# A four-layer attention and expert kernel on one core: the start reordered. Weight loads, folds and the normalisation of three contexts

## The chip, the cores and the metric

One core of one Trainium2 chip runs the whole program. The metric is the device time of one execution in microseconds, taken as the median of several runs. The engines are named as the profile names them: PE is TensorE (PEld its weight loads), DVE is VectorE, ACT is ScalarE, POOL is GpSimd, SP is SyncE, which here only issues DMAs.

## The reference, cut to what matters

Four sublayers follow each other on `x` (16 sequences of 128 tokens, 256 wide), each added to `x` after a layer norm: a cross attention on a context (16 x 128 x 192), a slot feed-forward, a second cross attention with 16 heads, and a mixture of 8 experts. Only the first one is touched by the change:

```python
def _L0_xattn_ref(modality1, modality2, ln1_g, ln1_b, ln2_g, ln2_b, Wq, bq, Wk, bk, Wv, bv, Wo, bo):
    ...
    x1 = layernorm(modality1, ln1_g, ln1_b)
    x2 = layernorm(modality2, ln2_g, ln2_b)
    q = x1 @ Wq + bq
    k = x2 @ Wk + bk
    v = x2 @ Wv + bv
    scores = jnp.einsum('bqe,bke->bqk', q, k) * scaling
    attn = jax.nn.softmax(scores, axis=-1)
    ctx = jnp.einsum('bqk,bke->bqe', attn, v)
    return ctx @ Wo + bo
...
x = x + _L0_xattn_ref(_layernorm(x, axis=-1), ctx_768, ...)
```

## The kernel before, in words

All of it is fp32. The 16 sequences are worked in four groups of four (`g` 0 to 3). Each group's rows `X[g]` and context `CH[g]` come by one DMA each; DVE takes mean and variance, POOL the power -0.5 (`root`), DVE normalises; PE transposes rows and context (`turn_x`, `turn_context`), ACT copies the transposes out of PSUM.

**Folding.** Weights that follow each other are multiplied once at the start: `Wq Wk^T` becomes `qk` (`fold_query`), `Wv Wo` becomes `vo` (`fold_value`), and the biases and the norm's gains go with them. So a group's attention is `query` (rows times `qk`, evicted by ACT to `Q`), `score` against the normalised context, softmax, `value` and `attend`. `fold_query` on PE has two parts that are interleaved by half: 256-column products of `WqT` and `WkT` into PSUM bank 4, and one-column products of `Wq` with the bias column `ln1_b` (from `keep`) into bank 5. `fold_query_bias` multiplies the result of the latter, `u_col`, by `WkT`. `fold_value` likewise has 256-column products of `WvT` and `Wo` and one-column ones of `Wv`.

**Order.** There is no planner. Each engine's program is a list of calls written out by hand in its block, and engines meet by semaphores. SP's list (L335 to L350) issues the loads in the order in which the queue shall work on them: the three matrices of the query fold (`WqT`, `WkT`, `Wq`: 768 KB), the first piece of `keep` (identity, ones, columns: 149.5 KB), the rows of group 0, the three of the value fold (768 KB), then contexts and rows by turns. The semaphore of each load is in the call. The counters `fold_ps` (PE has finished a fold) and `fold_ok` (DVE has read it out of PSUM and written it) count the folds in the order of the lists.

**PE's list (L1301 on).** It begins with `idle(5)`: five 128x256 matmuls on a zeroed tile `blank` whose results nobody reads. Then it waits for `keep`, runs `fold_query`, `fold_value`, one more idle matmul, `turn_x(0)`, `fold_query_bias`, `query(0)`, `fold_slot_values`, `turn_context(0)`, `turn_x(1)`, `fold_value_bias`, `score(0)`, `query(1)`, `value(0, 0)`, `turn_context(1)`, `turn_probs(0)`, `fold_slot_bias`, `turn_x(2)`, `score(1)` and so on. The helper `mm` (L923) records all matmuls, `turn` (L927) all transposes, so blocks are told apart by tiles and counts: an fp32 matmul is two records of MATMUL (and two of LDWEIGHTS), a 128x128 transpose one. A block of four 256-column matmuls is "128x256 x8"; it is what `fold_slot_values` (18.03 us) and `value` are; the 16 records at 19.84 us are `turn_context(0)` and `turn_x(1)`.

**DVE's list (L2131 on).** `stats_x(0)`, `fold_query` (the column `u_col`), `norm_x(0)`, `stats_c(0)`, `fold_query_bias` (the column `q_col`), `stats_x(1)`, `norm_c(0)`, `norm_x(1)`, `fold_value`, `stats_c(1)`, `fold_slots`, `most(0)`, `fold_value_bias`, `norm_c(1)`, `stats_x(2)`, `stats_c(2)`, `norm_x(2)`, `stats_c(3)`, `fold_slot_bias`, `most(1)`, `stats_x(3)`, `norm_c(2)`, and later `norm_c(3)`. `norm` (L1611) is four `tensor_scalar` instructions with a mean and a factor for each row of the tile.

**POOL's list (L444 on).** A few memsets, then nothing but `root` until 125 us; ahead of the second attention it has `spread_keys`.

**ACT's list (L712 on).** It waits for `keep`, fills `spread`, then `fold_query` (scales `qk` out of PSUM), `rows_turned(0)` (L545), `query(0)` (L565), `context_turned(0)` (L549), and so on.

The functions that the diff touches, as they stand before:

Of the kernel before, what the change touches and what calls it, by code (L numbers as in the profile page):

```python
# [61 lines left out]
])  # L62
FOLD_A, FOLD_B, FOLD_C = FOLD["Wo"][0], FOLD["fwv"][0], FOLD["whh"][0]
ROWS, ROWS_N = columns([
# [4 lines left out]
def build(nc, x_d, ctx_d, ctxT_d, keep_d, fold_d, rows_d, w13_d, w2_d, xh_d, early_d, out_d):  # L69
    with ExitStack() as stack:  # L70
# [3 lines left out]
        def sem(name):  # L74
            return stack.enter_context(nc.semaphore(name))
# [158 lines left out]
        keep_in, fold_in, rows_in = sem("keep_in"), sem("fold_in"), sem("rows_in")  # L234
        keep_in2, keep_in3, fold_in2, fold_in3, fold_in4 = (sem(t) for t in ("keep_in2", "keep_in3", "fold_in2", "fold_in3", "fold_in4"))
        x_in = [sem(f"x_in{g}") for g in range(NG)]
        c_in = [sem(f"c_in{g}") for g in range(NG)]
# [72 lines left out]
        def _(sp):  # L310
# [23 lines left out]

            some_fold(0, FOLD_A, fold_in)  # L335
            some_keep(0, KEEP_A, keep_in)
            rows_of(0)
            some_fold(FOLD_A, FOLD_B, fold_in2)
# [49 lines left out]
        def _(pool):  # L388
            def root(g, name):
                pool.wait_ge(s["var_" + name], g + 1)  # L390
                v = var["c" if name == "ch" else "x", g]
                pool.tensor_tensor(v[:, :], v[:, :], minus_half[:, :], ALU.pow).then_inc(s["rs_" + name], 1)  # L392

            def spread_keys(u):
# [57 lines left out]
            root(1, "xh")  # L452
            root(1, "ch")
            root(2, "xh")
            root(2, "ch")
            root(3, "ch")
            root(0, "xh2")
            root(3, "xh")
# [461 lines left out]
        def _(pe):  # L920
# [332 lines left out]
            def fold_query():  # L1253
                pe.wait_ge(fold_in, 16)
                for m in range(KD):
                    mm(ps[:, 4, m * D:(m + 1) * D], [(WqT[:, k, m * P:(m + 1) * P], WkT[:, k, :]) for k in range(KD)])
                    ins = mm(ps[:, 5, m:m + 1], [(Wq[:, k, m * P:(m + 1) * P], kept("ln1_b")[:, k:k + 1]) for k in range(KD)])
                ins.then_inc(fold_ps, 1)
# [6 lines left out]

            def fold_value():
                pe.wait_ge(fold_in2, 16)
                for m in range(KD):
                    mm(ps[:, 6, m * D:(m + 1) * D], [(WvT[:, k, m * P:(m + 1) * P], Wo[:, k, :]) for k in range(KD)])
                    ins = mm(ps[:, 7, 8 + m:9 + m], [(Wv[:, k, m * P:(m + 1) * P], kept("ln2_b")[:, k:k + 1]) for k in range(KD)])  # L1270
                ins.then_inc(fold_ps, 1)

# [28 lines left out]
            pe.wait_ge(set_ok, 2)  # L1301
            idle(5)
            pe.wait_ge(keep_in, 16)
            fold_query()
            fold_value()
            idle(1)
            turn_x(0)
            fold_query_bias()
            query(0)
            fold_slot_values()  # L1310
            turn_context(0)
            turn_x(1)
            fold_value_bias()
            score(0)
            query(1)
# [284 lines left out]
        def _(dve):  # L1600
# [33 lines left out]
            def norm_c(g):  # L1634
                norm(g, CH[g], CH[g], DC, "ch")
# [438 lines left out]
            def fold_query_bias():  # L2074
                dve.wait_ge(fold_ps, 3)
                dve.tensor_tensor(q_col[:, :], ps[:, 7, 0:KD], kept("ln2_g"), ALU.mult)
                folded()
# [65 lines left out]
            fold_value_bias()  # L2143
            norm_c(1)
            stats_x(2)
# [5 lines left out]
            stats_x(3)  # L2151
            norm_c(2)
            add_attention(0, 0)
# [3 lines left out]
            norm_x2(0)  # L2157
            norm_c(3)
            add_attention(1, 0)
# [288 lines left out]
```

## Time and profile before

| | |
|---|---|
| median of 3 runs | 548.62 us (548.39 to 549.3) |
| the profiled execution's own time | 548.08 us |
| its span, first to last instruction | 546.3 us, mean granted clock 0.999 |
| busy: PE, PEld, DVE, ACT, POOL | 97%, 80%, 52%, 47%, 31% of the span |
| DMA | 74.30 MB, mean 136 GB/s |

The profile is of one execution. Busy time is the sum of an engine's instructions; for PE their ends are modelled, so that two consecutive blocks overlap by about the length of one instruction in the rows, and the distance from start to start is the time that a block takes. A timeline row merges consecutive instructions of one kind and gives the start, the length, and in brackets the idle time before it with what ended it.

### The profile page before, as it was taken

To read this page: it belongs to the slowest core of one execution; us is meant where nothing else is said; L and a number is where in the kernel's file an instruction comes from. 1 tells how busy PE (TensorE), PEld (TensorE's weight loads), DVE (VectorE), ACT (ScalarE), POOL (GpSimd) and SP (SyncE) were. 2 spreads that over 40 slices of the span, in tenths; PEclk is the share of its full clock that TensorE was granted. 3 is DMA by queue.
4 is the path that set the end of the run, shared out by engine and by line. 5 is a ranking of instruction groups with operands and counts; after the bars stand their busy time and mean duration, and the time that the engine had idled before them with its cause. 6 is when DMAs were issued, how large, how long until landed. Compare 5 with 4: busy or idle time off the path is not lost.

```text
span 546.3 us, 11013 instructions
## 1 busy us (share of the span) xinstructions
PE 532.3 (97%) x3939; PEld 438.2 (80%) x3940; DVE 282.3 (52%) x843; ACT 255.3 (47%) x591; POOL 168.4 (31%) x152
## 2 busy tenths in 40 slices
PE   8999999999999999999999799999999999999996
PEld 7687878767555677767777589999999999999995
DVE  3886777988442776855788765722212121212110
ACT  2433676453356766688787825532221212222221
POOL 2221000102063221342222053345344444444423
PEclk9999999999999999999999999999999999999999
DMA  9930000000120000300460667978888888888832
GB/s 311 396 135 2 2 0 2 1 1 1 38 67 1 2 2 1 117 1 2 157 268 7 232 207 259 273 213 279 206 268 220 255 223 250 227 246 231 241 66 29
DMA packets 29083, 74.30 MB, mean 136 GB/s; under 512 B 5648, under 2 KB 20368, under 8 KB 23920
## 3 DMA queue, kind: packets, MB, share of 16 engines
q1 hardware_dynamic: 19456, 62.27, 32.4%
q0 software_dynamic: 7488, 10.39, 11.2%
q10 hardware_dynamic: 2096, 1.08, 0.7%
q8 instruction: 25, 0.41, 0.3%
q14 instruction: 18, 0.15, 0.1%
HBM read 62.88 MB, written 10.85 MB: 135 GB/s over the span
## 4 chain that ended last, share of the span: by engine, by line
PE 91%; ACT 3%; DVE 2%; DMA 1%; issue 1%; DVEq 0%; POOL 0%; SPq 0%
PE ps L923 62%; PE ps L1226 12%; PE ps L927 11%; PE ps L1074 1%; PE ps L1083 1%; DMA ring<-in_fold 1%; PE ps L1086 1%; ACT ring L645 1%; PE ps L1077 1%; PE ps L1014 1%; PE ps L1057 1%; ACT ring L652 1%; ACT ring L686 0%; ACT HF L657 0%; DVE arena L1615 0%
## 5 line engine op out<-in xcount | busy, mean ns | idle before, releaser
L923 PE MATMUL ps<-keep,arena 128*128 128x128 f32 (+2 forms) x976 | 114.9, 274 | 0.0
L923 PEld LDWEIGHTS ps<-keep,arena 128*128 128x128 f32 x976 | 112.8, 192 | 1.5 <-issue 1.1
L2053 DVE TENSOR_TENSOR keep<-keep,ps 128x512 f32<-128x512 f32 x39 | 26.8, 688 | 147.9 <-PE ps L923 139.9
L441 POOL DMA_INDIRECT out_x<-arena,row_no x38 | 59.9, 1576 | 101.1 <-ACT arena L704 82.3
L1226 PE MATMUL ps<-arena,keep 128*128 x312 | 73.7, 380 | 0.1
L693 ACT COPY keep<-ps 128x256 f32<-128x256 f32 x39 | 14.5, 372 | 105.5 <-PE ps L927 105.5
L400 POOL TENSOR_TENSOR ring<-arena,keep 128x512 f32<-128x512 f32 x32 | 33.4, 1047 | 97.0 <-PE ps L923 79.8
L1226 PEld LDWEIGHTS ps<-arena,keep 128*128 128x128 f32 x312 | 56.4, 190 | 6.6 <-issue 0.3
L645 ACT ACTIVATE ring<-ps,mx 128x128 f32<-128x128 f32 x192 | 52.1, 403 | 6.2 <-DVE mx L1753 6.2
L923 PE MATMUL ps<-ring,arena 128*32 128x128 f32 (+1 forms) x640 | 53.1, 348 | 1.5 <-ACT ring L652 1.4
L392 POOL TENSOR_TENSOR var_x<-var_x,minus_half 128x4 f32<-128x4 f32 x16 | 16.6, 1041 | 110.1 <-DVE var_x L1609 110.1
L923 PE MATMUL ps<-arena,keep 128*128 128x256 f32 (+1 forms) x144 | 44.2, 454 | 0.5 <-ACT arena L599 0.5
L652 ACT COPY ring<-ps 128x1024 f32<-128x1024 f32 x32 | 33.2, 1039 | 16.5 <-PE ps L927 15.9
L697 ACT ACTIVATE keep<-ps 128x512 f32<-128x512 f32 x39 | 23.3, 596 | 35.7 <-PE ps L923 35.6
L1753 DVE TENSOR_REDUCE mx<-ps 128x8 f32<-128x1024 f32 x24 | 29.2, 1216 | 17.9 <-PE ps L923 17.7
L927 PEld LDWEIGHTS ps<-keep,ring 128*128 128x128 f32 x256 | 28.2, 141 | 11.8 <-issue 8.4
L923 PE MATMUL ps<-keep,w_first 128*128 128x128 f32 x320 | 37.7, 275 | 0.0
L923 PEld LDWEIGHTS ps<-keep,w_first 128*128 128x128 f32 x320 | 36.7, 192 | 0.1
L923 PEld LDWEIGHTS ps<-ring,arena 128*32 128x32 f32 (+1 forms) x640 | 22.6, 124 | 17.3 <-issue 14.3
L923 PEld LDWEIGHTS ps<-arena,keep 128*128 128x128 f32 x144 | 26.4, 190 | 12.4 <-issue 9.5
L927 PE MATMUL ps<-keep,ring 128*128 128x128 f32 x256 | 34.2, 277 | 1.4 <-ACT arena L662 1.1
L428 POOL DMA_INDIRECT keep<-normed,row_no x30 | 30.3, 1010 | 10.9 <-issue 8.2
(266 smaller groups left out, 802.1 us busy)
## 6 DMA issues: line engine op xcount, KB each, us to landing
arena<-in_w SPq DMA_DIRECT2D x29, 1024.0 KB, 5.2
w_first<-in_w SPq DMA_DIRECT2D x10, 1024.0 KB, 5.3
arena<-in_w SPq DMA_DIRECT2D x8, 512.0 KB, 7.3
keep<-in_keep SPq DMA_DIRECT2D x1, 2827.0 KB, 17.0
ring<-in_fold SPq DMA_DIRECT2D x3, 768.0 KB, 7.0
arena<-in_x SPq DMA_DIRECT2D x4, 512.0 KB, 9.2
arena<-in_ctxT SPq DMA_DIRECT2D x4, 512.0 KB, 10.2
arena<-in_ctx SPq DMA_DIRECT2D x4, 384.0 KB, 9.4
```

What stands on the lines that cost most here:

```text
L392: pool.tensor_tensor(v[:, :], v[:, :], minus_half[:, :], ALU.pow).then_inc(s["rs_" + name], 1)
L400: pool.tensor_tensor(KB[u % 2], KT[g][:, t, bb * S:(bb + 1) * S].unsqueeze(1).broadcast_to([P, HT4, S]), kept("head_mask").unsqueeze(2).br ...
L428: pool.indirect_dma_start(out=XI[t % DEEP], out_offset=None, in_=early_d if t < EARLY else xh_d, in_offset=bass.IndirectOffsetOnAxis(ap=ro ...
L441: pool.indirect_dma_start(out=out_d, out_offset=bass.IndirectOffsetOnAxis(ap=rows_at, axis=0), in_=YO[t % DEEP], in_offset=None, compute_o ...
L645: ins = act.activation(PP[u % 2][:, h, :], scores_of(u)[:, h, :], ACT.Exp, bias=mx[u % 2][:, h:h + 1], scale=1.0)
L652: act.copy(PQ[u % 2], ps[:, 4:6, :].rearrange("p t (h n) -> p (t h) n", h=4)).then_inc(s["pt"], 1)
L697: act.activation(HA[r % 2], ps[:, 2 * (r % 2), :], ACT.Silu).then_inc(silu, 1)
L923: ins = pe.matmul(out, w, m, start=(k == 0), stop=(k == len(pairs) - 1))
L927: return pe.transpose(out, t, ident)
L1226: ins = pe.matmul(Y_PS[r % 2], HA[r % 2][:, k * P:(k + 1) * P], w2e[:, bass.ds(at + k * D, D)], start=(k == 0), stop=(k == INTER // P - 1))
L1753: dve.tensor_reduce(mx[u % 2][:, :], scores_of(u), AXX, ALU.max, negate=True).then_inc(s["neg"], 1)
L2053: dve.tensor_tensor(HA[r % 2], HA[r % 2], ps[:, 2 * (r % 2) + 1, :], ALU.mult).then_inc(act_ok, 1)
```

## The change

- **Loads.** The first fold load is cut in two: `WqT` and `WkT` (512 KB) go first, then the rows of group 0, then the first piece of `keep`, then `Wq` (256 KB, its own semaphore `fold_in_u`). The rest of SP's order stays.
- **The query fold on PE** is cut the same way: `fold_query` has only the 256-column products and waits only for the first load; `fold_query_row` has the one-column products, waits for `keep` and `fold_in_u`, and counts `fold_ps`.
- **The value fold on PE** is two calls: half `m=0` ahead of `turn_x(0)`, half `m=1` behind `query(0)`, with a wait for `fold_ok` 2 (DVE has read `q_col` from the same bank). DVE's `fold_query_bias` waits for `fold_ps` 2 now, since the value fold is counted third.
- **PE's order**: idle(4), `fold_query`, idle(1), `fold_query_row`, idle(2), `fold_value(0)`, `turn_x(0)`, `fold_query_bias`, `query(0)`, `fold_value(1)`, `turn_context(0)`, `turn_x(1)`, `fold_slot_values`, `score(0)`, `fold_value_bias`, `query(1)`; from there as before.
- **Contexts 1 to 3** are normalised on POOL, right behind their `root`, no longer on DVE.

```diff
@@ -60,7 +60,7 @@
     ("WqT", KD * D), ("WkT", KD * D), ("Wq", KD * D), ("Wo", KD * D), ("WvT", KD * D), ("Wv", KD * D),
     ("fwv", KD * D), ("fwoT", KD * D), ("slots", KD * NSLOT), ("whh", KD * 3 * D),
 ])
-FOLD_A, FOLD_B, FOLD_C = FOLD["Wo"][0], FOLD["fwv"][0], FOLD["whh"][0]
+FOLD_U, FOLD_A, FOLD_B, FOLD_C = FOLD["Wq"][0], FOLD["Wo"][0], FOLD["fwv"][0], FOLD["whh"][0]
 ROWS, ROWS_N = columns([
     ("bo", D), ("slot_scale", NSLOT), ("b2", NSLOT), ("tau", 1), ("fbo", D), ("ab2", D),
 ])
@@ -233,6 +233,7 @@
 
         keep_in, fold_in, rows_in = sem("keep_in"), sem("fold_in"), sem("rows_in")
         keep_in2, keep_in3, fold_in2, fold_in3, fold_in4 = (sem(t) for t in ("keep_in2", "keep_in3", "fold_in2", "fold_in3", "fold_in4"))
+        fold_in_u = sem("fold_in_u")
         x_in = [sem(f"x_in{g}") for g in range(NG)]
         c_in = [sem(f"c_in{g}") for g in range(NG)]
         y_in = [sem(f"y_in{g}") for g in range(NG)]
@@ -332,9 +333,10 @@
             def some_fold(lo, hi, landed):
                 sp.dma_start(ring[:, lo:hi], fold_d[:, lo:hi]).then_inc(landed, 16)
 
-            some_fold(0, FOLD_A, fold_in)
+            some_fold(0, FOLD_U, fold_in)
+            rows_of(0)
             some_keep(0, KEEP_A, keep_in)
-            rows_of(0)
+            some_fold(FOLD_U, FOLD_A, fold_in_u)
             some_fold(FOLD_A, FOLD_B, fold_in2)
             context_rows_of(0)
             rows_of(1)
@@ -391,6 +393,13 @@
                 v = var["c" if name == "ch" else "x", g]
                 pool.tensor_tensor(v[:, :], v[:, :], minus_half[:, :], ALU.pow).then_inc(s["rs_" + name], 1)
 
+            def norm_c(g):
+                pool.wait_ge(s["rs_ch"], g + 1)
+                for t in range(GB):
+                    ins = pool.tensor_scalar(CH[g][:, t, 0:DC], CH[g][:, t, 0:DC], mv["c", g][:, t, 0:1], var["c", g][:, t:t + 1],
+                                             ALU.subtract, ALU.mult)
+                ins.then_inc(s["ch"], 1)
+
             def spread_keys(u):
                 g, bb, t = u // UNITS, u // 2 % GB, u % 2
                 if u % UNITS == 0:
@@ -451,9 +460,12 @@
             root(0, "ch")
             root(1, "xh")
             root(1, "ch")
+            norm_c(1)
             root(2, "xh")
             root(2, "ch")
+            norm_c(2)
             root(3, "ch")
+            norm_c(3)
             root(0, "xh2")
             root(3, "xh")
             root(1, "xh2")
@@ -1254,6 +1266,11 @@
                 pe.wait_ge(fold_in, 16)
                 for m in range(KD):
                     mm(ps[:, 4, m * D:(m + 1) * D], [(WqT[:, k, m * P:(m + 1) * P], WkT[:, k, :]) for k in range(KD)])
+
+            def fold_query_row():
+                pe.wait_ge(keep_in, 16)
+                pe.wait_ge(fold_in_u, 16)
+                for m in range(KD):
                     ins = mm(ps[:, 5, m:m + 1], [(Wq[:, k, m * P:(m + 1) * P], kept("ln1_b")[:, k:k + 1]) for k in range(KD)])
                 ins.then_inc(fold_ps, 1)
 
@@ -1263,12 +1280,14 @@
                     ins = mm(ps[:, 7, m:m + 1], [(WkT[:, k, m * P:(m + 1) * P], u_col[:, k:k + 1]) for k in range(KD)])
                 ins.then_inc(fold_ps, 1)
 
-            def fold_value():
+            def fold_value(m):
                 pe.wait_ge(fold_in2, 16)
-                for m in range(KD):
-                    mm(ps[:, 6, m * D:(m + 1) * D], [(WvT[:, k, m * P:(m + 1) * P], Wo[:, k, :]) for k in range(KD)])
-                    ins = mm(ps[:, 7, 8 + m:9 + m], [(Wv[:, k, m * P:(m + 1) * P], kept("ln2_b")[:, k:k + 1]) for k in range(KD)])
-                ins.then_inc(fold_ps, 1)
+                if m:
+                    pe.wait_ge(fold_ok, 2)
+                mm(ps[:, 6, m * D:(m + 1) * D], [(WvT[:, k, m * P:(m + 1) * P], Wo[:, k, :]) for k in range(KD)])
+                ins = mm(ps[:, 7, 8 + m:9 + m], [(Wv[:, k, m * P:(m + 1) * P], kept("ln2_b")[:, k:k + 1]) for k in range(KD)])
+                if m:
+                    ins.then_inc(fold_ps, 1)
 
             def fold_slot_values():
                 pe.wait_ge(fold_in3, 16)
@@ -1299,19 +1318,21 @@
                 ins.then_inc(fold_ps, 1)
 
             pe.wait_ge(set_ok, 2)
-            idle(5)
-            pe.wait_ge(keep_in, 16)
+            idle(4)
             fold_query()
-            fold_value()
             idle(1)
+            fold_query_row()
+            idle(2)
+            fold_value(0)
             turn_x(0)
             fold_query_bias()
             query(0)
-            fold_slot_values()
+            fold_value(1)
             turn_context(0)
             turn_x(1)
+            fold_slot_values()
+            score(0)
             fold_value_bias()
-            score(0)
             query(1)
             value(0, 0)
             turn_context(1)
@@ -2072,7 +2093,7 @@
                 folded()
 
             def fold_query_bias():
-                dve.wait_ge(fold_ps, 3)
+                dve.wait_ge(fold_ps, 2)
                 dve.tensor_tensor(q_col[:, :], ps[:, 7, 0:KD], kept("ln2_g"), ALU.mult)
                 folded()
 
@@ -2141,7 +2162,6 @@
             fold_slots()
             most(0)
             fold_value_bias()
-            norm_c(1)
             stats_x(2)
             stats_c(2)
             norm_x(2)
@@ -2149,13 +2169,11 @@
             fold_slot_bias()
             most(1)
             stats_x(3)
-            norm_c(2)
             add_attention(0, 0)
             add_attention(0, 1)
             gather_stats(0, "xh2")
             fold_state()
             norm_x2(0)
-            norm_c(3)
             add_attention(1, 0)
             most(2)
             add_attention(1, 1)
```

## Rows read from the trace of the kernel before

**Rows 1.** Top of the page: the span, and the busy time of each engine

```profile
span 546.3 us, 11013 instructions
...
PE 532.3 (97%) x3939; PEld 438.2 (80%) x3940; DVE 282.3 (52%) x843; ACT 255.3 (47%) x591; POOL 168.4 (31%) x152
```

**Rows 2.** What TensorE waited for in 0 to 50 us: total, times, longest (us)

```profile
PE ps L927 <- DVE arena L1615: 0.8, 1, 0.8
...
PE ps L923 <- DMA ring<-in_fold: 0.8, 1, 0.8
```

**Rows 3.** Busy time by engine in 33 to 95 us, granted clock, DMA share, GB/s

```profile
33.00:95.00 62.00, 61.96 (x367) 50.30 (x368) 45.27 (x175) 34.23 (x70) 5.19 (x6) 1.00 0.01 1
```

**Rows 4.** DMA issues, first weight transfer and first rows: KB, us to landing

```profile
ring<-in_fold SPq DMA_DIRECT2D x1, 768.0 KB, 4.4
...
arena<-in_x SPq DMA_DIRECT2D x1, 512.0 KB, 5.5
```

**Rows 5.** Timeline to 15 us, SP's first issue and TensorE: start, length, instructions

```profile
0.73 0.39 SPq L333 DMA_DIRECT2D ring<-in_fold  x1
...
1.26 4.54 PE L923 MATMUL ps<-blank 128*128 128x256 f32 x10 [1.26 <-POOL blank L446]
...
5.60 0.73 PEld L923 LDWEIGHTS ps<-ring 128*128 128x128 f32 x4 [0.43 <-DMA keep<-in_keep]
...
9.13 0.73 PEld L923 LDWEIGHTS ps<-ring 128*128 128x128 f32 x4 [0.84 <-DMA ring<-in_fold]
...
11.75 0.30 PEld L923 LDWEIGHTS ps<-blank 128*128 128x128 f32 x2
...
12.08 1.01 PEld L927 LDWEIGHTS ps<-keep,arena 128*128 128x128 f32 x8
...
14.49 0.30 PEld L923 LDWEIGHTS ps<-arena,qk 128*128 128x128 f32 x2 [0.46 <-issue]
```

**Rows 6.** Timeline, VectorE and ScalarE on the first group of rows

```profile
7.15 1.40 DVE L1622 BATCH_NORM_STATS2 stat_x<-arena 128x6 f32<-128x256 f32 x4 [7.15 <-DMA arena<-in_x]
...
10.41 1.38 DVE L1615 TENSOR_SCALAR arena<-arena,mv_x,var_x 128x256 f32<-128x256 f32 x4 [0.84 <-POOL var_x L392]
...
13.37 1.01 ACT L545 COPY arena<-ps 128x1024 f32<-128x1024 f32 x1 [4.11 <-PE ps L927]
...
18.30 1.45 ACT L565 ACTIVATE arena<-ps,q_col,keep 128x512 f32<-128x512 f32 x2 [3.92 <-PE ps L923]
```

**Rows 7.** Timeline, TensorE from 18 to 34 us

```profile
18.03 1.89 PE L923 MATMUL ps<-ring 128*128 128x256 f32 x8
...
19.84 1.94 PE L927 MATMUL ps<-keep,arena 128*128 128x128 f32 x16
...
21.62 1.03 PE L923 MATMUL ps<-ring,spread 128*128 128x256 f32 x4
...
22.48 1.95 PE L923 MATMUL ps<-arena 128*128 128x128 f32 x16
...
24.27 3.60 PE L923 MATMUL ps<-arena,qk 128*128 128x512 f32 x8
...
33.04 1.09 PE L927 MATMUL ps<-keep,arena 128*128 128x128 f32 x8 [0.78 <-DVE arena L1615]
```

**Rows 8.** Timeline, VectorE around the second context's normalisation

```profile
24.47 0.69 DVE L1648 TENSOR_REDUCE nm<-ps 128x4 f32<-128x512 f32 x1 [0.34 <-PE ps L923]
...
26.71 1.24 DVE L1615 TENSOR_SCALAR arena<-arena,mv_c,var_c 128x192 f32<-128x192 f32 x4
...
31.61 1.38 DVE L1615 TENSOR_SCALAR arena<-arena,mv_x,var_x 128x256 f32<-128x256 f32 x4
```

**Rows 9.** GpSimd: two square roots in the timeline, and a group of the page

```profile
22.79 1.01 POOL L392 TENSOR_TENSOR var_c<-var_c,minus_half 128x4 f32<-128x4 f32 x1 [5.05 <-DVE var_c L1609]
...
31.78 1.25 POOL L392 TENSOR_TENSOR var_c<-var_c,minus_half 128x4 f32<-128x4 f32 x1 [0.73 <-DVE var_c L1609]
...
L400 POOL TENSOR_TENSOR ring<-arena,keep 128x512 f32<-128x512 f32 x32 | 33.4, 1047 | 97.0 <-PE ps L923 79.8
```

## The prediction, made before the changed kernel was run

> **What bounds the kernel now.** The page comes first: TensorE is busy for 532.3 of 546.3 us [rows 1]. A change to the start can only bring what TensorE loses there, so the next view is what it waited for in the first 50 us: 0.8 us for the transposes of the third group of rows, where VectorE was late, and 0.8 us for the value fold's weights [rows 2]. The timeline adds 0.43 us ahead of the query fold, where `keep` was late, 0.46 us ahead of `query(0)`, and idle matmuls: five at the start, one at 11.75 us [rows 5]. That is about 2.5 us of waits and 0.4 us of filler after 5.6 us; everything from 33 to 95 us is full: 61.96 us of 62.00 [rows 3]. Two questions decide: how many of these waits go, and what new ones the new order makes. I follow TensorE from block to block; a block costs the distance from its start to the next one's.
>
> **Prices.** Four 256-column matmuls: 19.84 - 18.03 = 1.81 us; sixteen transposes: 21.62 - 19.84 = 1.78; `fold_value_bias`: 22.48 - 21.62 = 0.86; `score`: 24.27 - 22.48 = 1.79 [rows 7]. The whole value fold is 11.75 - 9.13 = 2.62, so half of it is 1.31 and the one-column products of a fold are 2.62 - 1.81 = 0.81. `query(0)` is 18.03 - 14.49 = 3.54 [rows 5, 7]. An idle matmul takes 4.54 / 5 = 0.9 at the start, where TensorE runs at half its later pace, and 0.33 (weight loads) to 0.5 later; I take 0.43 [rows 5].
>
> **The loads.** 768 KB landed at 0.73 + 4.4 = 5.13, `keep` at 5.60, the rows at 1.65 + 5.5 = 7.15 [rows 4 to 6]. 512 KB of rows thus took 7.15 - 5.60 = 1.55 us. The first piece is now 256 KB shorter and lands about 0.8 earlier, at 4.4. The rows have 405.5 KB less ahead of them, 1.2 us: they land at 5.95. `keep` follows at 6.4 and `Wq` at 7.2. The value weights have the same bytes ahead of them as before and stay at 9.13. SP's one more issue costs 0.39 [rows 5]; the queue still has bytes to move, so I count it at nothing. Without that cover all later loads come 0.4 later.
>
> **TensorE to the value fold.** idle(4) ends at 1.26 + 0.8 x 4.54 = 4.9; the fold weights are there. `fold_query` starts then, at half pace until 5.6 (where the pace rose before), so 0.7 us do 0.35 of its 1.81, and it ends at 7.05. idle(1) 7.5; `fold_query_row` finds its weights, 8.3; idle(2) 9.15. `fold_value(0)` can start at 9.13 as before. So the 0.43 and 0.8 of waits have turned into filler and gained nothing by themselves. What is gained is that only half of the value fold stands ahead of the rows: TensorE is free at 10.45.
>
> **The first rows.** VectorE and GpSimd need 10.41 + 1.38 - 7.15 = 4.64 us from landing to `norm_x(0)`'s end [rows 6]; the two bias instructions fit in the wait for the root as before, since `fold_query_row` is done at 8.3. So the rows are ready at 10.6, and `turn_x(0)` starts there, not at 12.08 [rows 5]. From its start to `query(0)` were 14.49 - 12.08 = 2.41 us, of which ACT's copy and the turns are the chain and `fold_query_bias` lies beside [rows 5, 6]. `query(0)` starts at 13.0, 1.5 earlier. This is the change's real gain.
>
> **What comes late next.** `turn_context(0)` waits for `Q`, which ACT had 18.30 + 1.45 - 14.49 = 5.26 after `query(0)` began [rows 5, 6]: 18.25 now. TensorE has been free of `query(0)` since 16.55, and the only filling is `fold_value(1)`, 1.31, to 17.85. A new wait of 0.4 us stands where `fold_slot_values` (1.81) covered it fully. `fold_value(1)` itself waits for `fold_ok` 2; VectorE has then only `stats_c(0)` and the column behind it to do after 10.6, and 6 us for it. `turn_context(0)` starts at 18.25 against 19.84, 1.6 earlier [rows 7].
>
> **The debts.** Then come 1.78 (turns), 1.81 (`fold_slot_values`, moved behind), 1.79 (`score(0)`): `score(0)` ends at 23.65 against 24.27; `fold_value_bias` 0.86: `query(1)` starts at 24.5 against 24.27 [rows 7]. The 1.6 is spent: 1.31 on the deferred half of the fold, 0.4 on the new wait. Up to here the change is worth nothing, or costs 0.2.
>
> **GpSimd's share.** VectorE's list loses `norm_c(1)`, 1.24 us, from 26.71 to where `stats_x(2)` begins [rows 8]. `most(0)` starts with the end of `score(0)`, 0.65 earlier (24.47 before). So `norm_x(2)`, which ended at 31.61 + 1.38 = 32.99, ends at 32.99 - 0.65 - 1.2 = 31.15 [rows 8]. TensorE would be ready for `turn_x(2)` at 33.04 - 0.78 + 0.2 = 32.45 [rows 7], so its wait of 0.78 is gone and the start is 0.6 earlier than 33.04. GpSimd's four instructions aren't in the trace. Lower bound: VectorE's own, 1.24 for the four [rows 8]. Upper: the 128x512 product of two tensors, 1.047 each, 4.2 [rows 9]. I take 1.6, nearer the first because they are 192 wide with one tensor read. `root(1, "ch")`, at 22.79 before, starts near 21.7, since the value fold on VectorE starts when `fold_value(1)` ends and not at 19. `norm_c(1)` is then done between 23.9 and 26.9; `turn_context(1)` stands behind `query(1)` (3.4) and `value(0, 0)` (1.8), at 29.7: covered at either bound. Behind it on GpSimd's queue is `root(2, "xh")`, due near 28: also free. `norm_c(2)` and `norm_c(3)` replace VectorE work (some 2.5 us) in a stretch where TensorE doesn't wait [rows 3]: nothing.
>
> **One rule against it.** While VectorE ran `norm_x(2)`, GpSimd's root took 1.25 us, not 1.01, and VectorE's four took 1.38, as at 10.41 us where GpSimd was idle [rows 6, 8, 9]: in these rows only GpSimd pays. By them the sum keeps its 0.6. The Trainium skill, SBUF — State Buffer, "Who interferes with whom", says that the port pair which VectorE shares with GpSimd is an exclusive lock: whoever issues first holds it for a whole instruction and the other fully blocks. By that rule, VectorE could be the one that waits; that is the second rival.
>
> **The sum.** 0.6 us from 548.08 is 547.5 for a profiled execution; the median of the runs shown is 0.54 above the profiled one, so I expect a median of 548.62 - 0.6 = 548.0. A measurement of this kernel can tell about 0.2% (1.1 us) from no change: this is "same". The forecast's own range is a gain of 0 to 1.0.
>
> **Rivals.**
> 1. Faster. VectorE is relieved of 3.7 us (three times 1.24) and the new order closes the 0.4 us wait: the gain is 0.6 + 0.4, and up to 0.5 more if stalls behind the modelled ends of matmuls were VectorE's. Gain 1.0 to 1.5, 547.3. For it: TensorE at 97% hides small waits in its rows [rows 1]. Against: rows 3 are full, and `Q`'s chain is ACT's.
> 2. Slower, by the lock. If GpSimd's `norm_c` runs beside `norm_x(2)`, each of its four instructions may wait for one of GpSimd's, up to 1.047 [rows 9]: 4.2 us. `norm_x(2)` has 32.45 - 31.15 = 1.3 us of slack, so it decides from there and costs up to 2.9; net 2.3 slower, 550.9. Against: `norm_c(1)` would have to last until 29.8, 1.8 us each, and `norm_c(2)` starts only behind `root(2, "ch")`, near 31.3, when `norm_x(2)` is done.
> 3. Slower, by the clock. The profile prints a granted clock of 1.00 throughout [rows 3], but the first idle matmuls took twice the later time [rows 5]. If the pace rises one such stretch later in the new order, at about 10 us, the work from 5.6 on takes double: 1.46 + 0.4 + 0.8 + 0.9 ends near 11.3, not 9.15, and all after it moves by 2.0: net 1.4 slower, 550.0. It decides once the pace rises after 6. Against: TensorE is at work from 1.26 on in both.
> 4. The rows land no earlier, since transfers share the queues. Then `turn_x(0)` starts at 11.8 and everything behind moves by 1.2: 0.6 slower than before, 549.2.
>
> **Chances.** The forecast 0.60, rival 1 0.22, rival 4 0.08, rivals 2 and 3 0.05 each. Rival 1 is the only one below -0.2%, rivals 2 and 3 lie above +0.2%: faster 0.22, same 0.68, slower 0.10. The range goes from rival 1's middle, 547.0, to rival 4, 549.3; what is left out is the rest of rival 1 and rivals 2 and 3.
>
> **What would show it.** Right: rows landing near 6.0; `query(0)` near 13.0; a wait of some 0.4 for ACT ahead of `turn_context(0)`; `query(1)` within 0.3 of 24.27; `turn_x(2)` near 32.4 without a wait; GpSimd's instructions at 0.3 to 1.0 us. Wrong: a wait ahead of `turn_context(1)` or `turn_x(2)`, long VectorE instructions in `norm_x(2)`, idle matmuls at 0.9 after 6 us, or a difference that first appears after 33 us.

## The result, and the profile after

The changed kernel takes 548.02 us (median of 22 runs, 547.63 to 548.57) against 548.62 us (22 runs) before: ratio 0.9983, 95% interval 0.9977 to 0.9990. The medians differ by 0.60 us, less than the 0.2% that the prediction calls "same"; the ratio is one of means and stands for 0.9 us, since a few runs before took up to 551.23. Its profiled execution took 547.71 us. The top of its page, against [rows 1]:

```profile
span 545.9 us, 11019 instructions
...
PE 532.5 (98%) x3941; PEld 438.3 (80%) x3942; DVE 279.1 (51%) x831; ACT 255.5 (47%) x591; POOL 180.6 (33%) x164
```

VectorE has 3.2 us less to do, GpSimd 12.2 us more; TensorE has what it had, in 0.4 us less.

The landings first. DMA issues of the changed kernel, each from a window around its issue: the query fold's two matrices (issued at 0.74), the rows (1.19), `keep` (1.66), `Wq` (2.20), the value fold's weights (2.7); size and microseconds to landing.

```profile
ring<-in_fold SPq DMA_DIRECT2D x1, 512.0 KB, 4.1
...
arena<-in_x SPq DMA_DIRECT2D x1, 512.0 KB, 5.1
...
keep<-in_keep SPq DMA_DIRECT2D x1, 149.5 KB, 5.1
...
ring<-in_fold SPq DMA_DIRECT2D x1, 256.0 KB, 5.2
...
ring<-in_fold SPq DMA_DIRECT2D x1, 768.0 KB, 6.7
```

They land at 4.8, 6.36, 6.8, 7.4 and 9.4 us. What TensorE waited for in the first 50 us, to be held against [rows 2]:

```profile
PE ps L939 <- issue: 0.4, 1, 0.4
PE ps L935 <- ACT arena L557: 0.4, 1, 0.4
PE ps L935 <- DMA ring<-in_fold: 0.2, 1, 0.2
PE ps L939 <- DVE arena L1636: 0.2, 1, 0.2
```

And its timeline, with the instructions that decide on the other engines (start, length, instructions, idle time before):

```profile
4.88 1.59 PEld L935 LDWEIGHTS ps<-ring 128*128 128x128 f32 x8 [0.56 <-DMA ring<-in_fold]
...
9.42 0.73 PEld L935 LDWEIGHTS ps<-ring 128*128 128x128 f32 x4 [0.28 <-DMA ring<-in_fold]
...
11.07 0.86 PEld L939 LDWEIGHTS ps<-keep,arena 128*128 128x128 f32 x8 [0.27 <-DVE arena L1636]
...
13.33 0.30 PEld L935 LDWEIGHTS ps<-arena,qk 128*128 128x128 f32 x2 [0.46 <-issue]
...
17.14 1.45 ACT L577 ACTIVATE arena<-ps,q_col,keep 128x512 f32<-128x512 f32 x2 [3.92 <-PE ps L935]
...
18.68 1.94 PE L939 MATMUL ps<-keep,arena 128*128 128x128 f32 x16 [0.45 <-issue]
...
23.12 4.00 POOL L399 TENSOR_SCALAR arena<-arena,mv_c,var_c 128x192 f32<-128x192 f32 x4
...
24.84 3.60 PE L935 MATMUL ps<-arena,qk 128*128 128x512 f32 x8
...
30.22 1.38 DVE L1636 TENSOR_SCALAR arena<-arena,mv_x,var_x 128x256 f32<-128x256 f32 x4
...
32.67 1.04 PE L939 MATMUL ps<-keep,arena 128*128 128x128 f32 x8
```

Read it against [rows 5 to 8]. `turn_x(0)` starts at 11.07 (12.08 before) and `query(0)` at 13.33 (14.49). ACT finishes `Q` at 18.59, and `turn_context(0)` starts at 18.68, after 0.45 us in which TensorE has nothing to do: the new wait. (The bracket says "issue", that is, the view names no releaser; that it is `Q` follows from the code, where `turn_context(0)` waits for it, from the time, and from e3 below, where other work fills the gap.) `query(1)` then starts at 24.84 where it started at 24.27, so the reordering has cost 0.57 us by there. `turn_x(2)` has no bracket: VectorE was done with `norm_x(2)` at 31.60, and the 0.78 us wait at 33.04 is gone. From the next block on the shift is constant. `score(1)`, and `gate_r(1)` of the slot layer, which stands behind ACT's copy of the second group's shares, first in the changed kernel, then before:

```profile
33.54 1.95 PE L935 MATMUL ps<-arena 128*128 128x128 f32 x16
...
95.34 1.99 PE L935 MATMUL ps<-arena,keep 128*128 128x256 f32 x8 [0.46 <-ACT arena L611]
```

```profile
33.97 1.95 PE L923 MATMUL ps<-arena 128*128 128x128 f32 x16
...
95.78 1.99 PE L923 MATMUL ps<-arena,keep 128*128 128x256 f32 x8 [0.46 <-ACT arena L599]
```

That is 0.43 and 0.44 us. I use the second row, `gate_r(1)`, below as the mark of what a start is worth.

### The profile page after: what moved, and what is told of

Read it like the earlier page. It is cut to its first block, busy times and chain, and to the rows that moved or that the text cites. A ratio compares the mean times of both kernels' runs of the same rounds, so it can differ in the third digit from the quotient of the medians.

```text
span 545.9 us, 11019 instructions
## 1 busy us (share of the span) xinstructions
PE 532.5 (98%) x3941; PEld 438.3 (80%) x3942; DVE 279.1 (51%) x831; ACT 255.5 (47%) x591; POOL 180.6 (33%) x164
## 4 chain that ended last, share of the span: by engine, by line
PE 91%; ACT 4%; DVE 2%; issue 1%; DMA 1%; POOL 0%; DVEq 0%; SPq 0%
PE ps L935 62%; PE ps L1238 12%; PE ps L939 11%; ACT ring L657 2%; PE ps L1086 1%; PE ps L1095 1%; DMA arena<-in_x 1%; ACT ring L664 1%; PE ps L1098 1%; PE ps L1089 1%; PE ps L1026 1%; PE ps L1069 1%; ACT HF L669 0%; ACT ring L698 0%; PE ps L1167 0%
## 5 line engine op out<-in xcount | busy, mean ns | idle before, releaser
L1774 DVE TENSOR_REDUCE mx<-ps 128x8 f32<-128x1024 f32 x24 | 29.2, 1216 | 17.5 <-PE ps L935 17.3
```

The lines of the kernel that those rows point to most:

```text
L1774: dve.tensor_reduce(mx[u % 2][:, :], scores_of(u), AXX, ALU.max, negate=True).then_inc(s["neg"], 1)
```

## Experiments

Each kernel's times are compared with runs of the kernel before on the same chip in the same session; its median there lay between 548.45 and 549.06. Where two kernels come from different sessions, the difference of their medians is therefore uncertain by some tenths. I then compare what each gains on the kernel before in its own session (0.60 for the changed kernel), and the marks. A mark is one execution, and the first loads alone land up to 0.25 us earlier or later from one profile to the next.

### The two halves of the change, each alone

```diff
@@ e1, against the kernel before: only GpSimd's part
             root(1, "ch")
+            norm_c(1)
             root(2, "xh")
             root(2, "ch")
+            norm_c(2)
             root(3, "ch")
+            norm_c(3)
...
-            norm_c(1)
...
-            norm_c(2)
...
-            norm_c(3)
```

(and GpSimd's function `norm_c` as in the change).

> The kernel before, with one part of the change: GpSimd normalises contexts 1 to 3; loads, folds and TensorE's order stay as they were. Theory A (the reordering is worth nothing or less, the gain is the 0.78 us wait ahead of turn_x(2) that VectorE's relief removes): turn_x(2)'s weight loads start at 31.9 us, where TensorE is free, and not at 33.04; score(1) follows at 32.9 and not 33.87, so the kernel is 1.0 us faster than before (547.6) and 0.4 faster than the whole change. Theory B (the gain is the earlier first query): 0.0 to 0.2 us faster than before, with a wait somewhere ahead of 33 us that takes the place of the one removed. Theory C (GpSimd's four take 4.0 us instead of 1.24 and make turn_context(1) or the root of x2 late): slower than before, with a wait for POOL.

547.51 us, ratio 0.9969 (0.9956 to 0.9983); against the 548.87 of the same session it is 1.4 us faster, against the 548.62 above 1.1. Its timeline, TensorE, `query(1)`, `turn_x(2)` and the mark:

```profile
24.04 3.60 PE L933 MATMUL ps<-arena,qk 128*128 128x512 f32 x8
...
31.87 1.04 PE L937 MATMUL ps<-keep,arena 128*128 128x128 f32 x8
...
94.55 1.99 PE L933 MATMUL ps<-arena,keep 128*128 128x256 f32 x8 [0.46 <-ACT arena L609]
```

The mark is 1.23 us earlier than before and 0.79 earlier than in the changed kernel. (0.2 of it are loads that happened to land earlier: the value fold's matmuls started at 8.91, and 9.14 before.) Without them the removed wait is worth 1.0 us. This one part of the change, alone, is worth about twice the whole.

```diff
@@ e2, against the changed kernel: the reordering without GpSimd's part
-            norm_c(1)
...
-            norm_c(2)
...
-            norm_c(3)
@@ and on VectorE's list
             fold_value_bias()
+            norm_c(1)
             stats_x(2)
```

(`norm_c(2)` and `norm_c(3)` go back to their places too.)

> The changed kernel with the contexts' normalisation back on VectorE: the reordering alone. Theory A: query(1)'s weight loads at 24.6 us as in the changed kernel (24.16 before), norm_x(2) ends 1.2 later than the changed kernel's 31.6, so turn_x(2) waits for VectorE until 32.9 and starts 0.1 earlier than before; time within 0.2 us of before (548.6). Theory B: it keeps the whole 0.6 us of the change (548.0).

548.22 us, ratio 0.9989 (0.9980 to 0.9998), 0.65 faster than before in its session: the number of theory B, though not by way of an earlier `query(1)`. VectorE and TensorE around `turn_x(2)`, then the mark:

```profile
26.28 1.24 DVE L1626 TENSOR_SCALAR arena<-arena,mv_c,var_c 128x192 f32<-128x192 f32 x4
...
31.18 1.38 DVE L1626 TENSOR_SCALAR arena<-arena,mv_x,var_x 128x256 f32<-128x256 f32 x4
...
32.61 1.09 PE L929 MATMUL ps<-keep,arena 128*128 128x128 f32 x8
...
95.34 1.99 PE L925 MATMUL ps<-arena,keep 128*128 128x256 f32 x8 [0.46 <-ACT arena L601]
```

The mark stands at 95.34, exactly where the whole change has it. I had expected VectorE to hold `turn_x(2)` until 32.9. It was done at 32.56, because `score(0)` comes earlier in the new order and `most(0)` with it, just when TensorE, 0.6 us late, was ready. So the two parts remove the same wait: either is enough, and with the reordering in place GpSimd's part adds next to nothing: nothing at the mark, or 0.13 if one counts that `turn_x(0)` happened to start 0.13 earlier here; and by the times 0.60 in one session against 0.65 in the other. Theory A, which had this run no faster than before, failed. But the reordering is not what makes the change worth having either, since it earns 0.44 against GpSimd's 1.23.

### The wait for Q ahead of `turn_context(0)`

```diff
@@ e3, against the changed kernel
             fold_value(1)
+            fold_slot_values()
             turn_context(0)
             turn_x(1)
-            fold_slot_values()
             score(0)
```

> The changed kernel with fold_slot_values ahead of turn_context(0) again, right behind fold_value(1). If TensorE's idle 0.45 us ahead of turn_context(0) (it waits for Q) is a net loss of the new order, it is gone, query(1) and everything behind it start 0.45 earlier, and the kernel is 0.45 us faster than the changed one (547.6). Rival: the next thing to be late (the second query's eviction, or VectorE's value bias ahead of value(0,0)) takes it back: under 0.15 us.

548.02 us, the same as the changed kernel (0.85 faster than before in its session, not 0.60, but with the mark at 95.35). The rival was right in its size and not in what it named: neither the second query's eviction nor the value bias took the gain back. The wait for Q is gone, but `score(0)` now stands directly behind the turns and has this bracket:

```profile
22.11 2.02 PE L935 MATMUL ps<-arena 128*128 128x128 f32 x16 [0.32 <-ACT arena L561]
```

That is ACT's copy of the transposed context. `query(1)` starts at 24.84 as in the changed kernel. The next attempt covers both waits, with half of the block in each:

```diff
@@ e7, against the changed kernel
-            def fold_slot_values():
+            def fold_slot_values(m):
                 pe.wait_ge(fold_in3, 16)
-                for m in range(KD):
-                    mm(ps[:, 4, m * D:(m + 1) * D], ...)
+                mm(ps[:, 4, m * D:(m + 1) * D], ...)
...
             fold_value(1)
+            fold_slot_values(0)
             turn_context(0)
             turn_x(1)
-            fold_slot_values()
+            fold_slot_values(1)
             score(0)
```

> The changed kernel with fold_slot_values in halves: one ahead of turn_context(0), in TensorE's wait for Q, one ahead of score(0), in the wait for the context's copy. Theory: the run with the whole of it in front lost its 0.45 us again to a 0.32 us wait for ACT's copy ahead of score(0); in halves (0.9 us each) both waits are covered, query(1) starts at 24.4 instead of 24.84, and the kernel is 0.45 us faster than the changed one (547.6). Rival: something else holds query(1) or value(0,0), and it stays within 0.15 us of it (548.0).

547.59 us, ratio 0.9985 (0.9976 to 0.9994). That is 0.43 below the changed kernel's median, but only 0.26 more than its gain in the session of each, and the two ratios can't be told apart; so the times alone don't show a gain on the changed kernel. The trace does. Both waits have left the table of waits, and `query(1)` and the mark are

```profile
24.54 3.60 PE L935 MATMUL ps<-arena,qk 128*128 128x512 f32 x8
...
95.05 1.99 PE L935 MATMUL ps<-arena,keep 128*128 128x256 f32 x8 [0.46 <-ACT arena L611]
```

0.30 and 0.29 earlier, although the value fold happened to start 0.2 later than in the changed kernel.

### The rows' place in the queue

```diff
@@ e6, against the changed kernel: the old loads, one transfer of three matrices
-            some_fold(0, FOLD_U, fold_in)
-            rows_of(0)
+            some_fold(0, FOLD_A, fold_in)
             some_keep(0, KEEP_A, keep_in)
-            some_fold(FOLD_U, FOLD_A, fold_in_u)
+            rows_of(0)
...
-                pe.wait_ge(fold_in_u, 16)
```

> The changed kernel with the loads of the kernel before: WqT, WkT and Wq in one transfer, keep, then the rows; TensorE's new order and GpSimd's part stay. Theory L (the rows' landing sets the start of the new order one to one): rows land at 7.15 as before, turn_x(0) at 11.8 and not 11.07, so 0.75 us slower than the changed kernel (548.8) and 1.2 slower than GpSimd's part alone (547.5). Rival M: with the value fold's weights back at 8.9 to 9.1 (9.4 in the changed kernel) half of it is won back: 0.3 slower (548.3).

548.73 us, ratio to before 1.0005 (0.9996 to 1.0014): the gain of the whole change is gone. TensorE waits for the rows ahead of `turn_x(0)`,

```profile
11.84 1.09 PE L937 MATMUL ps<-keep,arena 128*128 128x128 f32 x8 [0.61 <-DVE arena L1633]
```

which starts there and not at 11.07; `query(1)` starts at 25.60 and the mark is 96.11, 0.77 later than in the changed kernel, as theory L had it (0.7 by the medians, 0.9 by the gains in each session). The new order pays for the rows' landing one to one; the old order hid it behind the whole value fold.

The other way to put the rows back, keeping the cut, did something that I had not foreseen.

```diff
@@ e4, against the changed kernel
             some_fold(0, FOLD_U, fold_in)
-            rows_of(0)
+            some_fold(FOLD_U, FOLD_A, fold_in_u)
             some_keep(0, KEEP_A, keep_in)
-            some_fold(FOLD_U, FOLD_A, fold_in_u)
+            rows_of(0)
```

> The changed kernel with the first rows loaded behind Wq and keep, in the old order of bytes. Rows land at 7.2 us instead of 6.36. My working: turn_x(0) then starts at 11.85 instead of 11.07, and the 0.8 us goes through Q's eviction to turn_context(0) and all the rest: 0.8 us slower than the changed kernel (548.8). Rival: the value fold's weights bound the start (they land at 9.4 whichever comes first), and half of the delay or more is swallowed: 0 to 0.4 us slower.

553.91 us, the median of six runs from 550.07 to 554.73: 5.0 slower than before in its session, some 5.6 slower than the changed kernel. The rows landed at 9.65 us and the value fold's weights at 11.7, though the bytes ahead of them are those of the kernel before. TensorE waited 2.3 us, and then this happened (start, length):

```profile
11.73 1.23 PE L935 MATMUL ps<-ring 128*128 128x256 f32 x4 [2.33 <-DMA ring<-in_fold]
...
17.69 6.25 PE L935 MATMUL ps<-arena,qk 128*128 128x512 f32 x8
```

`query(0)` takes 6.25 us where it took 3.67. The granted clock by stretch (columns: stretch, its length, busy time of PE, PEld, DVE, ACT, POOL, granted clock, DMA share, GB/s):

```profile
10.00:12.00 2.00, 0.27 (x1) 0.27 (x2) 1.77 (x11) 0.00 (x0) 0.15 (x1) 1.00 1.09 354
12.00:14.00 2.00, 1.60 (x8) 1.36 (x7) 1.16 (x5) 0.00 (x0) 0.89 (x1) 0.66 1.07 385
14.00:16.00 2.00, 1.64 (x8) 1.64 (x9) 1.85 (x10) 0.00 (x0) 0.00 (x0) 0.50 1.03 378
...
22.00:24.00 2.00, 2.00 (x6) 0.91 (x5) 0.87 (x3) 0.00 (x0) 0.00 (x0) 0.78 1.28 462
```

From about 13 to 22.5 us the clock is granted at 0.50, the 1.2 GHz level, after a stretch in which TensorE was nearly idle. The one run of 550.07 us had a mean granted clock of 0.998, the five above 553 of 0.989 to 0.992. To split the loss, five more idle matmuls went into the wait:

```diff
@@ e8, against e4
-            idle(2)
+            idle(7)
             fold_value(0)
```

> The kernel with the rows behind Wq and keep (553.9 us), with seven idle matmuls ahead of fold_value(0) instead of two: five more fill the 2.3 us in which TensorE waited for the value fold's weights. Theory K (the 5.9 us it lost are 2.5 of late landing and the rest of TensorE's clock, granted at 0.50 from about 13 to 23 us after that wait): the clock stays at 1.00, only the landing is left, 550 to 551. Rival: the clock falls all the same, or the loss is the landing's alone: 553 or more.

550.60 us, 2.15 slower than before in its session: some 3 us faster than e4 for adding work. The landings are within 0.2 us of e4's, the mean granted clock of the execution is 0.999 and not 0.990, and `query(0)` takes its 3.67 again:

```profile
16.44 3.67 PE L935 MATMUL ps<-arena,qk 128*128 128x512 f32 x8 [0.41 <-ACT arena L557]
```

The marks are 95.34, 98.42 and 102.25 in the changed kernel, e8 and e4. So e4's loss is about half landing and half clock: 2.75 and 2.9 us by the gains in each session, 3.1 and 3.8 by these marks. Keeping the clock up across a wait is one thing that idle matmuls in this kernel can do. It is not rival 3 as it stands, which had the pace rise late at the start; here it fell after a wait.

The late landing was tried in the kernel before, without any other edit:

```diff
@@ e9, against the kernel before
-            some_fold(0, FOLD_A, fold_in)
+            some_fold(0, FOLD["Wq"][0], fold_in)
+            some_fold(FOLD["Wq"][0], FOLD_A, fold_in)
...
-                pe.wait_ge(fold_in, 16)
+                pe.wait_ge(fold_in, 32)
```

> The kernel before with one edit: its first transfer (WqT, WkT, Wq, 768 KB) is cut in two, 512 and 256 KB, in the same order of bytes. Theory P (the cut itself makes later transfers land late, as in the run with the rows last, where they landed at 9.65 and not 7.15): rows at 9 us or later, value weights after 11, some us slower. Theory Q (the slip comes from elsewhere): all landings within 0.3 us of before, time within 0.2 us of 548.6.

553.73 us, ratio 1.0102 (1.0064 to 1.0140). The first two pieces and `keep` land early (3.8, 4.1 and 4.1 us after their issues at 0.74, 1.2 and 1.65), then the rows, issued at 2.12, and the value weights, issued at 2.60, take

```profile
arena<-in_x SPq DMA_DIRECT2D x1, 512.0 KB, 7.1
...
ring<-in_fold SPq DMA_DIRECT2D x1, 768.0 KB, 8.8
```

against 5.5 and 7.0 before. TensorE waits 2.02 us and the clock falls here too, to 0.50 from about 11 to 17.5 us:

```profile
12.00:14.00 2.00, 2.00 (x9) 1.73 (x7) 1.52 (x5) 0.00 (x0) 0.45 (x1) 0.50 1.05 391
```

The median is of four runs, 551.21 to 557.00. Theory P holds: in the order of before the cut alone does it. In the changed kernel, which has the rows between the pieces, it doesn't occur. With `keep` between them:

```diff
@@ e11, against the kernel before
-            some_fold(0, FOLD_A, fold_in)
+            some_fold(0, FOLD["Wq"][0], fold_in)
             some_keep(0, KEEP_A, keep_in)
+            some_fold(FOLD["Wq"][0], FOLD_A, fold_in)
...
-                pe.wait_ge(fold_in, 16)
+                pe.wait_ge(fold_in, 32)
```

> The kernel before with its first transfer cut in two and keep between the two pieces: WqT and WkT, keep, Wq, rows. The cut with nothing between cost 5.1 us, as the rows landed at 9.2 and not 7.15. Theory P1 (two short weight transfers right behind each other are what makes the later ones slip): rows at 7.2 to 7.5, under 0.4 us slower than before. Theory P2 (a cut anywhere with the rows fourth does it): rows at 9 again and 4 us or more slower; then only the rows' place ahead of the second piece saves the changed kernel from it.

Four runs from 549.44 to 553.16 us, median 551.83. The profiled one is the fastest of the four: there the rows landed at 7.8 and the value weights at 10.0, TensorE waited 1.40 us and its clock stayed at 1.00. The two runs above 553 had a mean granted clock of 0.993, against 0.998 and 0.996 in the two faster ones; their landings are not known. Neither theory fits. It is not only two weight transfers in a row, and not always 2 us. Why a cut early in the queue delays the third and fourth transfer stays open; the rows before or between the pieces is the only order with a cut that was seen to be free of it.

### GpSimd beside VectorE

```diff
@@ e5, against the changed kernel: four instructions more on GpSimd
             root(2, "xh")
+            pool.wait_ge(s["rs_xh"], 3)
+            for t in range(GB):
+                pool.tensor_scalar(probe[:, t * DC:(t + 1) * DC], blank[:, 0:DC], mv["x", 2][:, t, 0:1], var["x", 2][:, t:t + 1],
+                                   ALU.subtract, ALU.mult)
             root(2, "ch")
```

> The changed kernel with four more tensor_scalar instructions on GpSimd (128x192, into a tile nobody reads) between the roots of x2 and of context 2, that is from 29.8 to 33.8 us, beside VectorE's norm_x(2) at 30.2. Theory S (GpSimd waits, VectorE doesn't): VectorE's four take 1.38 us as ever and turn_x(2) starts as before; context 2's normalisation moves 4 us back to 35.8 to 41.8, still ahead of turn_context(2) near 42.3; time within 0.2 us of the changed kernel (548.0). Rival R (the shared port pair is held for a whole instruction by whoever is first, and GpSimd's instructions take 1.0 us): VectorE's four are stretched to 2.4 to 5 us, turn_x(2) waits for VectorE, 0.5 to 3 us slower.

547.87 us, ratio to before 0.9990 (0.9981 to 1.0000), 0.59 faster than before in its session: no slower than the changed kernel.

```profile
29.77 4.19 POOL L468 TENSOR_SCALAR probe<-blank,mv_x,var_x 128x192 f32<-128x192 f32 x4
...
30.20 1.59 DVE L1641 TENSOR_SCALAR arena<-arena,mv_x,var_x 128x256 f32<-128x256 f32 x4
...
32.66 1.04 PE L944 MATMUL ps<-keep,arena 128*128 128x128 f32 x8
```

Side by side, GpSimd's four lose 0.2 us (3.98 to 4.19) and VectorE's four lose 0.2 (1.38 to 1.59). Nobody is held for a whole instruction of 1.0 us, and the 0.2 vanish in `norm_x(2)`'s slack. By the Trainium skill, SBUF — State Buffer, "Who interferes with whom", the loser of the shared port pair is blocked for the other's whole instruction when VectorE works in a mode that uses both of its ports; the trace doesn't agree if these instructions ran in such a mode, which no run here shows.

### A start that beats both

The readings say what the new order wants: the rows as early as can be, since their chain (landing, statistics, root, norm) is what TensorE waits for, and something useful in the 0.4 us of ACT's copy.

```diff
@@ e10, against e7
-            some_fold(0, FOLD_U, fold_in)
             rows_of(0)
+            some_fold(0, FOLD_U, fold_in)
...
-            idle(4)
+            idle(6)
             fold_query()
-            idle(1)
             fold_query_row()
-            idle(2)
-            fold_value(0)
+            idle(1)
             turn_x(0)
+            fold_value(0)
...
             stats_x(0)
-            fold_query()
             norm_x(0)
+            fold_query()
```

> The kernel with fold_slot_values in halves (547.6), with the rows loaded first of all and turn_x(0) ahead of fold_value(0); VectorE normalises the rows ahead of reading u_col; idle matmuls six, none, one instead of four, one, two. If the first rows' chain and the two waits it leaves on TensorE set the start: rows land at 4.8, WqT and WkT at 6.4, turn_x(0) starts at 9.5 and not 11.3, fold_value(0) covers ACT's copy, query(0) starts at 12.5 and not 13.6, query(1) at 23.6 and not 24.5: 0.9 us faster than that kernel, 546.7, and 1.9 faster than before. Rival (the value fold's weights at 9.4 hold the new order as much as the old): query(0) no earlier than 13.2, 547.3 or more.

546.50 us, ratio to before 0.9964 (0.9951 to 0.9978): 2.0 us faster than the kernel before in its session, and 1.1 better than e7. TensorE's table of waits for the first 60 us has one row left, the wait for the zeroed tile at 1.26. `turn_x(0)`, `query(0)`, `query(1)` and the mark:

```profile
9.67 1.04 PE L939 MATMUL ps<-keep,arena 128*128 128x128 f32 x8
...
12.67 3.68 PE L935 MATMUL ps<-arena,qk 128*128 128x512 f32 x8
...
23.62 3.60 PE L935 MATMUL ps<-arena,qk 128*128 128x512 f32 x8
...
94.12 1.99 PE L935 MATMUL ps<-arena,keep 128*128 128x256 f32 x8 [0.46 <-ACT arena L611]
```

The weights of the fold land at 5.6 there, and the idle matmuls hold TensorE until 6.5. One of them was taken out:

```diff
@@ e12, against e10
-            idle(6)
+            idle(5)
```

> The kernel with the rows first, with five idle matmuls ahead of the query fold instead of six. In that kernel the fold's weights landed at 5.6 us and the idle matmuls held TensorE until 6.5, and the rows were normalised at 9.0 while turn_x(0) started at 9.67. If the idle matmuls are what holds it: fold_query at 5.7, turn_x(0) at 9.05, everything behind it 0.6 us earlier, 545.9. Rival: the pace rises later in a run with less work, or fold_value(0)'s weights (9.0) or the 0.4 us for ACT's copy come into view: 546.3 or more.

546.71 us, ratio 0.9959 (0.9944 to 0.9973), not to be told from e10. The start is earlier as expected, `query(1)` at 23.07 and the mark at 93.57, 0.55 earlier. But the profiled span is 544.9 against e10's 544.7. The 0.55 are still there when GpSimd issues the first gather (312.46 against 313.02). They are lost in two places behind it. First the second transposes of gathered rows, e10 above and e12 below:

```profile
318.33 0.41 PE L939 MATMUL ps<-keep 128*128 128x128 f32 x2 [0.55 <-ACT keep L705]
...
318.01 0.41 PE L939 MATMUL ps<-keep 128*128 128x128 f32 x2 [0.79 <-DMA keep<-early,row_no]
```

TensorE waits here 0.55 us in the profiles of before, the changed kernel, e1, e3, e5 and e10, 0.73 to 0.79 in those of e2, e6, e7 and e12. The longer wait stands also in e6, whose start is the latest of these, so an earlier start is not needed for it. It takes 0.24 of the 0.55. Then the end. GpSimd's stores add rows into the output, and each waits for the one before to land. The last one in e10, and the last two in e12:

```profile
540.62 1.55 POOL L450 DMA_INDIRECT out_x<-arena,row_no  x1 [1.10 <-issue]
...
538.74 1.55 POOL L450 DMA_INDIRECT out_x<-arena,row_last  x1 [2.88 <-DMA out_x<-arena,row_no]
...
540.60 1.55 POOL L450 DMA_INDIRECT out_x<-arena,row_no  x1 [0.30 <-issue]
```

In e10 the last store follows VectorE's last instruction, at 539.45. In e12 that instruction is still 0.32 earlier, at 539.13, but GpSimd is busy until 540.29 with the store before, which had itself waited for a landing; the last one starts no earlier. The profiles of e1, e6 and e7 end in this way too, with 0.30 to 0.42 us ahead of the last store. What makes this chain of stores late in some profiles and not in others stays open. It can hide a few tenths of an earlier start.

## Why the prediction was right, point by point

**The number.** 548.0 was forecast and 548.02 measured, a gain of 0.6 and 0.60. That the hundredths agree is luck: the profiled execution came to 547.71 and not 547.5, the mark gives 0.44, the means of all runs 0.9. The two terms that make up the sum were both too small, and their errors offset each other for the most part. The wait ahead of `turn_x(2)` was put at 0.78 and is worth 1.0 when nothing else changes (e1). The debt at `query(1)` was put at 0.2 and was 0.57. 0.78 - 0.2 is the forecast 0.6; 1.0 - 0.57 = 0.43 is what the mark shows.

**The loads.** The term that failed by size is "they land at 5.95": 6.36 was measured, since the first 512 KB landed at 4.8 and not 4.4: a quarter-megabyte less brought 0.3 us and not 0.8 [rows 4, 5]. "The value weights ... stay at 9.13" was 9.42. Everything from `turn_x(0)` on was therefore 0.3 to 0.5 later than forecast: `turn_x(0)` 11.07 (10.6), `query(0)` 13.33 (13.0), `turn_context(0)` 18.65 (18.25). The half pace that the sum gave the query fold until 5.6 didn't occur: from its start at 4.89 to the next block were 1.83 us. In e2's profile they were 2.45. It made no difference to the value fold's start, which waited for its weights at 9.42.

**What comes late next.** Right: the new wait for `Q` was put at 0.4 and measured 0.45. e3 shows that covering it alone gains nothing at the mark; e7 shows 0.29 there, once the copy behind it is covered as well, with loads 0.2 later.

**The debts.** "Worth nothing, or costs 0.2" was 0.57 by the starts of `query(1)`; the difference is the late rows. The sign "`query(1)` within 0.3 of 24.27" therefore failed. The others on that list came about, the rows and `query(0)` 0.3 to 0.4 late.

**GpSimd's share.** `norm_x(2)` ended at 31.60 (31.15 forecast) and the wait of 0.78 went; `turn_x(2)` started at 32.45 by its weight loads, 32.67 by its matmuls (32.45 forecast). GpSimd's four took 4.0 us and not 1.6, near the upper bound of 4.2; `norm_c(1)` was done at 27.12 and needed near 30, so it cost nothing. What failed here is the account: I gave the whole gain to VectorE's relief. e2 shows that the reordering alone removes the same wait, and e1 that the relief alone is worth 1.23 at the mark: TensorE, not being late, could start `turn_x(2)` at 31.87. The change's parts are 1.23 and 0.44 alone and 0.44 together. I saw that the reordering was in debt at `query(1)` and didn't draw the conclusion that the kernel would be better without it.

**Rivals.** 1 (VectorE's 3.7 us bring more later): wrong, the shift is 0.43 at `score(1)` and 0.44 at 95 us. The range is also said to begin at this rival's middle, 547.0; a gain of 1.0 to 1.5 has its middle at 547.4. 2 (the lock): wrong by e5, 0.2 us instead of up to 4.2. 3 (the pace rises late at the start): didn't occur; e4, e8 and e9 show another case, a clock that falls after a wait, worth some 3 us in e4. 4 (the rows no earlier): e6 is that case, 548.73 where 549.2 was forecast.

## What to carry to other kernels

Before reordering the start of a kernel whose main engine is otherwise full, ask which wait the new order removes and what other edit would remove it without the debt; two edits that remove the same wait don't add up. A block moved out of the front of the queue is not saved, it comes back later, and moving a filler from one wait can open the next one (e3), so halve it and cover both (e7). Where transfers are late, a wait on TensorE can cost more than its length again in clock: here one of 2.3 us cost some 3 us more, and idle matmuls in it saved them.

## What the runs showed of the hardware

- After 2.0 to 2.3 us of waiting near 10 us, TensorE's clock was granted at 0.50 (1.2 GHz) for some 10 us in e4 and for some 6.5 us in e9; with idle matmuls in the wait (e8) it stayed at 1.00, and so it did after a wait of 1.40 us (e11, profiled execution).
- Cutting a 768 KB transfer in two, with the same bytes in the same order, made the following ones land 2 us later in the profiled execution (9.2 instead of 7.15, 11.4 instead of 9.1) and the kernel 5 us slower. The cause is open.
- A GpSimd `tensor_scalar` of 128x192 took 1.0 us, as much as the power of 128x4 elements (1.01) and the product of 128x512 (1.047); VectorE's took 0.31 apiece.
